# A pause of GpSimd's own between two row gathers and the next two, in the blocks of a graph layer with experts

## The chip, the cores and the metric

One core of one Trainium2 chip runs the whole kernel. The metric is the time of one execution on the device, in microseconds (us). Engines: TensorE (PE, matmuls; PEld its weight loads), VectorE (DVE), ScalarE (ACT), GpSimd (POOL) and SyncE (SP, which here only issues transfers).

## The reference

The inputs are 6250 nodes of 256 features and 200000 edges (source, destination, one of 32 relation types, a weight), sorted by destination. Cut to what matters:

```
xn = layernorm(x)
weight = einsum('rb,bio->rio', w_comp, bases)          # 32 relations from 8 bases
msg = (xn @ weight)[src, rel_type] * edge_weight
gnn = relu(segment_sum(msg, dst))
mix = linear attention over all nodes, layer norm, two dense layers, layer norm, + xn
x = x + gnn + mix
# 8 experts of three dense layers each, weighted by a softmax router, on layernorm(x)
out = x + ffn(layernorm(x))
```

## The kernel before, in words

**Edges as steps.** The sorted edges are cut into chunks of 128, and a chunk that touches several groups of 16 destination nodes is taken once for each. Each such piece is a step. For a step GpSimd gathers the 128 source rows of `xn` (128 x 1 KB) from DRAM into one of the 16 slots of `ring`; TensorE multiplies them with a matrix of 128 x 128 that VectorE has made (`selm`: destination in the group, times relation coefficients), in two halves of two products each; VectorE adds the PSUM result onto a running sum (`acc`, L1306), and SyncE stores every four sums to DRAM (`step_sums`). 16 steps are one iteration (UN = 16); there are 123 iterations, 1968 steps.

**Stages.** 7 iterations run beside the first stage of the mixing (M1_ITS), 8 beside its second stage for the first four tiles; these 15 are FIRST. Then come the blocks: 12 blocks of 9 iterations (BLK), 108 iterations. In a block the steps run between the mixing of the next four tiles of nodes, the product of the aggregated sums with the bases, and (from the second block on) the eight experts on the rows of the block before. Two more blocks without steps end the kernel.

**What sets the order.** Every engine has its own instruction list in an order written out by hand; between the engines there are only counting semaphores. Names that the prediction uses:
- `mm_done` counts multiplied steps and starts at 16, so GpSimd may gather step s + 16 into a slot once step s is multiplied.
- `idx_ready`: VectorE writes the row indices of iteration it + 1 (L1276, `indices`) after the first two accumulations of iteration it. GpSimd waits for it at the start of each iteration.
- `row_in0` to `row_in7`: one for each pair of slots. TensorE waits for a pair before it multiplies its even step (in `step`).
- `wait_apart` (L325) waits for a semaphore, and counts up another, `passed`, behind it.
- `const` on GpSimd is a `Chain`: each of the setup's iotas (L700) waits for the signal of the one before it.
- L1270 is VectorE's product that makes four steps' matrices (`select`); `h_low` (L1005) is the low part of the experts' hidden values. Both read two operands from SBUF.

GpSimd does little else than the gathers: constants at the start, 16 gathers of edge records, and then one loop of 41 turns with three iterations in each, since the index buffer has three parts (SETS = 3).

Of the kernel before, what the change touches and what calls it, by code (L numbers as in the profile page):

```python
# [13 lines left out]
P = 128  # L14
# [28 lines left out]
UN = 16  # L43
# [14 lines left out]
FIRST = M2_AT + 2 * SUP  # L58
ITERS = FIRST + (SUPERS - 1) * BLK
SETS = 3  # L60
# [19 lines left out]
def gps_layer(nc, x, src, dst, etype, eweight, bases, w_comp, Wq, Wk, Wv, Wm, W1, W2, g1, b1, g2, b2,  # L80
              Wr, br, fW1, fb1, fg1, fbe1, fm1, fv1, fW2, fb2, fg2, fbe2, fm2, fv2, Wo, bo, out):
    ctx = ExitStack()
    with ctx:
        sems = {}

        def sem(name):
            if name not in sems:
                sems[name] = ctx.enter_context(nc.semaphore(name))
            return sems[name]
# [3 lines left out]
        def sb(name, shape, dt=F32):  # L93
            place_of[name] = -(-nc.sbuf_base // 32) * 32
            return ctx.enter_context(nc.sbuf_tensor(name, shape, dt))
# [205 lines left out]
        last_i = sb("last_i", [P, 4], I32)  # L301
        zrow = sb("zrow", [P, KH * (P + 1)])
        flag = sb("flag", [1, 1], I32)
        flagf = sb("flagf", [P, 1])


# [18 lines left out]
        def wait_apart(eng, name, value):  # L325


            eng.wait_ge(sem(name), value)
            eng.sem_inc(sem("passed"), 1)
# [22 lines left out]
        def dma_ahead(eng, name, n):  # L352
            eng.dma_start(lead_s[:, 4 * n:4 * n + 4], x[0:1, 0:4]).then_inc(sem(name), DLEAD)
# [339 lines left out]
        @block.gpsimd  # L693
        def _(pool):
            dma_ahead(pool, "s_scat", len(LED_DMA))

            const = Chain(pool, "pool_const")

            def iota(o, pattern, cm=0):
                const(pool.iota(o, pattern, base=0, channel_multiplier=cm, allow_small_or_imprecise_dtypes=True))  # L700

            iota(iota16[:, :], [[1, GN]])
            iota(super_at[:, :], [[SGROUPS, SUPERS]])
            iota(group_no[:, :], [[P, 4]], 1)
            iota(super_no[:, :], [[1, SUPERS]])
            iota(chunk_no[:, :], [[P, CB]], 1)
            iota(slot_no[:, :], [[P, SB]], 1)
            for q in range(4):
                iota(relcol[32 * q:32 * q + 32, :], [[0, 1]], 1)
            pool.wait_ge(sem("dve_const"), 1)  # L710
            const(pool.affine_select(out=ident[:, :], in_=ident[:, :], compare_op=ALU.not_equal, fill=1.0, base=0,
                                     pattern=[[-1, P]], channel_multiplier=1))
            pool.wait_ge(sem("dve_const"), 8)

            const(pool.affine_select(out=rowmask[:, :], in_=rowmask[:, :], compare_op=ALU.is_gt, fill=0.0, base=NODES,
                                     pattern=[[-P, TILES]], channel_multiplier=-1))

            pool.wait_ge(sem("flag_ready"), 1)
            unsorted = pool.value_load(flag[0:1, 0:1], min_val=0, max_val=1)
            with pool.If(unsorted > 0):  # L720
                pool.iota(s_iota, [[1, SORTK]], base=0, channel_multiplier=0,
                          allow_small_or_imprecise_dtypes=True).then_inc(sem("s_const"), 1)
                pool.wait_ge(sem("s_fill"), 3)

                pool.affine_select(out=s_low, in_=s_low, compare_op=ALU.is_gt, fill=0.0, base=0,
                                   pattern=[[1, P]], channel_multiplier=-1).then_inc(sem("s_const"), 1)
                with pool.Fori(0, CHUNKS) as i:
                    wait_apart(pool, "s_recs", i + 1)
                    pool.indirect_dma_start(out=srt, out_offset=bass.IndirectOffsetOnAxis(ap=s_idx, axis=0),
                                            in_=s_rec, in_offset=None).then_inc(sem("s_scat"), 16)  # L730


            pool.wait_ge(sem("rec_ready"), 1)
            with pool.Fori(0, SB // 4) as i:
                for u in range(4):
                    wait_apart(pool, "col_ready", 8 * i + 2 * u + 2)
                    pool.indirect_dma_start(out=irec[:, u, :], out_offset=None, in_=rec,
                                            in_offset=bass.IndirectOffsetOnAxis(ap=colc[:, u:u + 1], axis=0)
                                            ).then_inc(sem(f"irec_in{u}"), 16)
            pool.wait_ge(sem("xn_ready"), 1)  # L740

            def steps(it, u):
                pool.wait_ge(sem("idx_ready"), it + 1)
                for k in range(UN):
                    wait_apart(pool, "mm_done", it * UN + k + 1)
                    pool.indirect_dma_start(out=ring[:, k, :], out_offset=None, in_=xnD,  # L746
                                            in_offset=bass.IndirectOffsetOnAxis(ap=idxc[:, u, k:k + 1], axis=0)
                                            ).then_inc(sem(f"row_in{k // 2}"), 16)

            with pool.Fori(0, ITERS // SETS) as i:  # L750
                for u in range(SETS):
                    steps(SETS * i + u, u)


        @block.scalar
        def _(act):
# [1268 lines left out]
```

## Time and profile before

| | |
|---|---|
| median of 3 runs | 4193.39 us (4190.02 to 4204.43) |
| the profiled execution | 4209.15 us |
| its span, first to last instruction | 4207.4 us |
| TensorE, weight loads busy | 80%, 70% of the span |
| VectorE, ScalarE, GpSimd busy | 54%, 19%, 46% |
| mean granted clock of TensorE | 0.92 of full speed |
| transfers | 864.29 MB, 205 GB/s on the mean |

Busy time is the sum of an engine's instructions, without its register, branch and semaphore instructions and without the issuing of transfers; the gathers, whose descriptors GpSimd itself writes, do count as its busy time. A transfer's own time in flight is not in it. "Idle before" is the time in which an engine did nothing just ahead of an instruction, put to what released it: "issue" where no waiting is seen, "remote" where the releaser is not in the records.

### The profile page before, as it was taken

To read this page: it belongs to the slowest core of one execution; us is meant where nothing else is said; L and a number is where in the kernel's file an instruction comes from. 1 tells how busy PE (TensorE), PEld (TensorE's weight loads), DVE (VectorE), ACT (ScalarE), POOL (GpSimd) and SP (SyncE) were. 2 spreads that over 40 slices of the span, in tenths; PEclk is the share of its full clock that TensorE was granted. 3 is DMA by queue.
4 is the path that set the end of the run, shared out by engine and by line. 5 is a ranking of instruction groups with operands and counts; after the bars stand their busy time and mean duration, and the time that the engine had idled before them with its cause. 6 is when DMAs were issued, how large, how long until landed. Compare 5 with 4: busy or idle time off the path is not lost.

```text
span 4207.4 us, 68614 instructions
## 1 busy us (share of the span) xinstructions
PE 3357.9 (80%) x18778; PEld 2955.5 (70%) x18778; DVE 2255.9 (54%) x6008; ACT 800.3 (19%) x1546; POOL 1949.4 (46%) x2001
## 2 busy tenths in 40 slices
PE   0179976686988889898898888888888888888887
PEld 0157765575877868788787787877877778777675
DVE  5634465555555565555555555555555555555422
ACT  0023420001112121121211212112121221211233
POOL 0132246655555555555555555555454555555100
PEclk9999987887999999999899998998989999899899
DMA  6467776666766667676676766767667676676532
GB/s 195 128 194 237 241 206 189 198 194 207 235 206 219 211 219 239 201 230 208 210 232 208 229 210 209 228 217 226 204 210 231 214 219 216 208 237 207 163 103 80
DMA packets 647245, 864.29 MB, mean 205 GB/s; under 512 B 63829, under 2 KB 524195, under 8 KB 646686
## 3 DMA queue, kind: packets, MB, share of 16 engines
q1 hardware_dynamic: 510962, 549.74, 40.0%
q0 software_dynamic: 95776, 262.27, 21.8%
q10 hardware_dynamic: 40140, 47.81, 3.4%
q8 instruction: 179, 2.93, 0.3%
q14 instruction: 188, 1.54, 0.1%
HBM read 551.97 MB, written 316.84 MB: 206 GB/s over the span
## 4 chain that ended last, share of the span: by engine, by line
PE 53%; issue 11%; DVE 9%; another core or an unknown queue 5%; ACT 3%; DVEq 1%; SPq 0%; DMA 0%; ACTq 0%
PE PS L1674 53%; DVE steps L1306 4%; ACT feed L926 1%; DVE steps L1270 1%; DVE feed L1602 1%; ACT h_high L925 0%; ACT mixbuf L902 0%; DVE h_low L1005 0%; PE PS L1743 0%; ACT mixbuf L896 0%; DVE lst L1415 0%; DVE mixbuf L1437 0%; DVE lnr L1005 0%; DVE mixbuf L1005 0%
## 5 line engine op out<-in xcount | busy, mean ns | idle before, releaser
L746 POOL DMA_INDIRECT steps<-normed_nodes,steps x1968 | 1931.2, 981 | 1781.9 <-PE PS L1674 877.3
L1306 DVE SCALAR_TENSOR_TENSOR steps<-steps,PS 128x256 f32<-128x256 f32 x1968 | 944.7, 480 | 1599.5 <-PE PS L1674 1107.1
L1674 PE MATMUL PS<-steps 128*128 128x128 f32 x7872 | 1267.4, 299 | 316.6 <-issue 133.3
L1674 PEld LDWEIGHTS PS<-steps 128*128 128x128 f32 x7872 | 1169.1, 211 | 422.6 <-issue 257.7
L926 ACT ACTIVATE feed<-PS,bnc 128x512 f32<-128x512 f32 x416 | 319.9, 774 | 825.5 <-PE PS L1674 547.4
L1674 PE MATMUL PS<-bases_s,feed 128*128 128x256 f32 x1664 | 440.7, 408 | 0.0
L1674 PEld LDWEIGHTS PS<-bases_s,feed 128*128 128x128 f32 x1664 | 416.4, 334 | 6.2
L1270 DVE TENSOR_TENSOR steps<-steps 128x512 f32<-128x512 f32 x494 | 337.3, 683 | 0.1
L1674 PE MATMUL PS<-w_one,feed 128*128 128x256 f32 (+1 forms) x1028 | 309.5, 427 | 5.8 <-ACT feed L926 5.8
L925 ACT ACTIVATE h_high<-PS,bnc 128x512 fp32r<-128x512 f32 x208 | 161.6, 777 | 794.5 <-PE PS L1674 724.4
L1674 PE MATMUL PS<-h_high,split_in 128*128 128x512 f32 x832 | 276.0, 458 | 16.8 <-ACT feed L926 16.7
L1674 PE MATMUL PS<-x1t_high,split_in 128*128 128x512 f32 x832 | 261.6, 439 | 2.7 <-DMA w_one<-in_L_ffn_Wo_dram 2.3
L1602 DVE SCALAR_TENSOR_TENSOR feed<-PS,rw,feed 128x256 f32<-128x256 f32 x416 | 181.6, 479 | 111.7 <-PE PS L1674 106.1
L1674 PE MATMUL PS<-w_zero,feed 128*128 128x256 f32 x832 | 226.6, 402 | 6.7 <-ACT feed L926 6.7
L1674 PEld LDWEIGHTS PS<-w_one,feed 128*128 128x128 f32 x1028 | 179.5, 193 | 46.0 <-issue 24.7
L1674 PEld LDWEIGHTS PS<-h_high,split_in 128*128 128x128 f32 x832 | 163.8, 217 | 47.2 <-ACT feed L926 21.3
L1674 PE MATMUL PS<-w_s,mixbuf 128*128 128x256 f32 x416 | 122.7, 446 | 87.5 <-ACT mixbuf L902 50.0
L1674 PEld LDWEIGHTS PS<-wblk,steps 128*128 128x128 f32 x992 | 141.1, 217 | 65.5 <-DVE feed L1524 34.9
L1674 PE MATMUL PS<-wblk,steps 128*128 128x32 f32 x992 | 143.6, 292 | 49.7 <-DVE feed L1524 30.2
L1674 PEld LDWEIGHTS PS<-x1t_high,split_in 128*128 128x128 f32 x832 | 153.2, 202 | 27.0 <-DMA w_one<-in_L_ffn_Wo_dram 2.7
L1674 PEld LDWEIGHTS PS<-w_zero,feed 128*128 128x128 f32 x832 | 154.0, 204 | 25.5 <-ACT feed L926 11.3
L1005 DVE TENSOR_TENSOR h_low<-feed,h_high 128x1024 fp32r<-128x1024 f32 x104 | 127.3, 1224 | 69.1 <-ACT feed L926 63.5
(208 smaller groups left out, 2881.3 us busy)
## 6 DMA issues: line engine op xcount, KB each, us to landing
step_sums<-steps SPq DMA_DIRECT2D x492, 512.0 KB
split_in<-expert_split SPq DMA_DIRECT2D x104, 1024.0 KB
feed<-step_sums SPq DMA_DIRECT2D x416, 128.0 KB
steps<-step_types SPq DMA_DIRECT2D x125, 256.0 KB
steps<-normed_nodes,steps POOLq DMA_INDIRECT x1968
mixbuf<-mix_hidden SPq DMA_DIRECT2D x53, 256.0 KB
w_zero<-in_L_ffn_Wo_dram SPq DMA_DIRECT2D x52, 256.0 KB
w_one<-in_L_ffn_Wo_dram SPq DMA_DIRECT2D x52, 256.0 KB
```

Of the source, the lines that this page charges most:

```text
L746: pool.indirect_dma_start(out=ring[:, k, :], out_offset=None, in_=xnD, in_offset=bass.IndirectOffsetOnAxis(ap=idxc[:, u, k:k + 1], axis=0) ...
L925: act.activation(h1_high[:, k, :], bank(b0 + k), ACT.Relu, bias=bias, scale=scale)
L926: act.activation(o[:, k, :], bank(b0 + k), ACT.Relu, bias=bias, scale=scale).then_inc(sem(f"f_h{s}"), 1)
L1005: return dve.tensor_tensor(o, a, b, op)
L1270: dve.tensor_tensor(selm[:, q % 2, :, :, :], hot[:, s, :].unsqueeze(3).to_broadcast([P, BATCH, GN, BASES]), coef[:, s, :].unsqueeze(2).to_ ...
L1306: dve.scalar_tensor_tensor(acc[:, k % ACCR, :], acc[:, (k - 1) % ACCR, :], keepc[:, k:k + 1], PS[:, slot(k):slot(k) + C], ALU.mult, ALU.ad ...
L1602: dve.scalar_tensor_tensor(oacc[:, j, :], o_part(j), rw[:, EXPERTS * j + e:EXPERTS * j + e + 1], oacc[:, j, :], ALU.mult, ALU.add).then_in ...
L1674: return pe.matmul(o, a, b, start=start, stop=stop)
```

## The change

A buffer `hold` of 128 x 8 words is added in SBUF. In `steps`, when `turn` is given, GpSimd does two things ahead of each even gather, behind the wait for `mm_done`: it clears `hold` with a memset that counts up the semaphore `held`, and waits until `held` has reached this memset's own number. Nothing reads `hold`. The one loop over all iterations becomes two: the first over FIRST = 15 iterations without `turn`, the second over the other 108 with it.

```diff
+        hold = sb("hold", [P, 8])
...
-            def steps(it, u):
+            def steps(it, u, turn=None):
                 pool.wait_ge(sem("idx_ready"), it + 1)
                 for k in range(UN):
                     wait_apart(pool, "mm_done", it * UN + k + 1)
+                    if turn is not None and k % 2 == 0:
+                        pool.memset(hold[:, :], 0.0).then_inc(sem("held"), 1)
+                        wait_apart(pool, "held", turn * (UN // 2) + k // 2 + 1)
                     pool.indirect_dma_start(out=ring[:, k, :], out_offset=None, in_=xnD,
                                             in_offset=bass.IndirectOffsetOnAxis(ap=idxc[:, u, k:k + 1], axis=0)
                                             ).then_inc(sem(f"row_in{k // 2}"), 16)
 
-            with pool.Fori(0, ITERS // SETS) as i:
+            with pool.Fori(0, FIRST // SETS) as i:
                 for u in range(SETS):
                     steps(SETS * i + u, u)
-
+            with pool.Fori(0, (ITERS - FIRST) // SETS) as i:
+                for u in range(SETS):
+                    steps(SETS * i + FIRST + u, u, SETS * i + u)
```

## Rows read from the trace of the kernel before

**Rows 1.** The page: GpSimd's busy time, and the shares of the chain by engine.
```profile
PE 3357.9 (80%) x18778; PEld 2955.5 (70%) x18778; DVE 2255.9 (54%) x6008; ACT 800.3 (19%) x1546; POOL 1949.4 (46%) x2001
...
PE 53%; issue 11%; DVE 9%; another core or an unknown queue 5%; ACT 3%; DVEq 1%; SPq 0%; DMA 0%; ACTq 0%
```

**Rows 2.** By line, L746: durations (ns), its idle time by releaser, who waited for it.
```profile
L746 POOL DMA_INDIRECT steps<-normed_nodes,steps x1968: 940/946/1991, 226.8 to 3924.3; - x197
...
  PE PS L1674: 877.3, 521
  issue: 440.5, 1298
  DVE steps L1276: 371.6, 96
...
  PEld PS L1674: 7.1, 1
  PE PS L1674: 6.9, 1
```

**Rows 3.** By line, L1306: durations (ns), first and last start (us).
```profile
L1306 DVE SCALAR_TENSOR_TENSOR steps<-steps,PS x1968: 461/481/483, 245.2 to 3952.8; 128x256 f32<-128x256 f32 x197
```

**Rows 4.** Windows by block, L746: stretch, its length, busy time (count), clock, DMA share, GB/s.
```profile
800.00:1036.00 236.00, 138.48 (x146) 0.80 0.66 203
1036.00:1302.00 266.00, 143.13 (x146) 0.92 0.69 216
...
sum 3151.00, POOL 1685.78; mean POOL 140.48
```

**Rows 5.** Timeline, all engines, 2041 to 2053 us: start, length, instructions [idle before, releaser].
```profile
2042.12 0.17 DVE L1276 CAST steps<-steps 128x16 int32 x1
...
2043.18 0.94 POOL L746 DMA_INDIRECT steps<-normed_nodes,steps  x1 [3.98 <-DVE steps L1276]
...
2044.43 0.94 POOL L746 DMA_INDIRECT steps<-normed_nodes,steps  x1 [0.30 <-issue]
...
2051.72 0.69 DVE L1270 TENSOR_TENSOR steps<-steps 128x512 f32<-128x512 f32 x1
...
2052.05 1.18 POOL L746 DMA_INDIRECT steps<-normed_nodes,steps  x1 [0.30 <-issue]
```

**Rows 6.** Timeline of GpSimd, the first 30 us.
```profile
0.30 0.10 POOL L2015 MEMSET const-float32-0.0<- 128x1 f32 x1 [0.30 <-issue]
...
1.36 0.70 POOL L353 DMA_DIRECT2D lead_s<-in_x_dram  x1 [0.85 <-POOLq L2015]
2.16 0.18 POOL L700 IOTA iota<- 128x16 f32 x1
2.41 0.16 POOL L700 IOTA super_at<- 128x13 f32 x1
...
4.35 0.29 POOL L711 TENSOR_SCALAR_AFFINE_SELECT ident<-ident 128x128 f32<-128x128 f32 x1 [0.16 <-DVE headmask L1045]
```

**Rows 7.** Transfers by line: count, size, median us from issue to landing.
```profile
mixbuf<-in_x_dram SPq DMA_DIRECT2D x8, 768.0 KB, 6.1
```

**Rows 8.** Groups of VectorE, 800 to 3951 us: busy us, mean ns, idle before.
```profile
L1270 DVE TENSOR_TENSOR steps<-steps 128x512 f32<-128x512 f32 x432 | 294.9, 683 | 0.1
...
L1005 DVE TENSOR_TENSOR h_low<-feed,h_high 128x1024 fp32r<-128x1024 f32 x88 | 107.7, 1224 | 5.6
```

**Rows 9.** Waits: who waited for whom, us in total, times, longest us.
```profile
DVE steps L1306 <- remote: 326.2, 82, 17.7
...
ACT feed L926 <- remote: 160.2, 18, 13.6
...
PE PS L1743 <- DMA feed<-in_x_dram: 4.3, 1, 4.3
...
PE PS L1674 <- DMA w_one<-in_L_ffn_Wo_dram: 2.3, 1, 2.3
```

## The prediction

> **What bounds the kernel now.** I read the chain of work that ended last first, because it says which engine's delay would count. TensorE carries 53% of it, issue time 11%, VectorE 9%, and GpSimd is not in it [rows 1]. GpSimd is busy for 46% of the span, nearly all of it with the gathers of line 746. So the change touches an engine off the path, and the question is how much it can be slowed before it comes onto it.
>
> The view by line for 746 gives both sides [rows 2]. Before the 1968 gathers GpSimd sat idle for 877.3 us waiting for TensorE to free a ring slot, for 371.6 us waiting for VectorE's next list of indices, and 440.5 us in short issue gaps. The other way round almost nobody waits for a gather: one weight load and one matmul, 7.1 and 6.9 us, in the whole run. Inside the first block the same view lists no waiter at all. The ring explains it: gather s+16 is issued as soon as step s is multiplied, so each gather has the time of nearly 16 steps to land. The last gather starts at 3924.3 us [rows 2] and the last accumulation, which uses it, at 3952.8 us [rows 3]: 28.5 us later.
>
> How fast the ring turns is read from the windows by block [rows 4]. Windows cut at the block borders hold 145 gathers or so; the twelve blocks take 3151 us for 1728 steps, so a pair of steps (one handshake in the new code) takes 3151/864 = 3.65 us. The first block, which has no experts, is the quickest: 236 us, 236/72 = 3.28 us a pair. These two are the rates GpSimd has to keep.
>
> **What the change adds.** Nothing is removed and no transfer is added or moved past another on a queue. In 108 iterations with 8 pairs each, 864 memsets are added, and 864 waits for the memset's own signal. The waits for `mm_done` and `idx_ready` stay. The one loop of 41 turns becomes two, of 5 and 36, with the same three iterations in each turn: one more loop start, counted as nothing. Behind the waiting memset only the next gather of the same engine is queued; behind that, TensorE, by `row_in`, 16 steps later.
>
> The price of one handshake, when GpSimd has slots in hand and does not wait for TensorE anyway. Before, gathers run back to back: 0.95 us of gather and 0.30 us to the next one [rows 5], so a pair takes 2.50 us; 1298 of the 1968 follow within such an issue gap [rows 2]. As a gather behind another starts after 0.30 us and one that waited for a signal only after 0.89 us (below), I take it that part of a gather's start is done ahead while the one before runs; the new wait stops that. The new sequence for a pair is
> - gather, gap, gather: 0.95 + 0.30 + 0.95 = 2.20 us;
> - the gap before the memset. After the one other DMA that GpSimd issues, which ends at 1.36 + 0.70 = 2.06 us, the next operation starts at 2.16 us [rows 6]: 0.10 us;
> - the memset of 128x8 words. None of this shape is in the trace; those of 128x1 take 0.10 us [rows 6]. 0.10 us;
> - from the memset's end to the next gather's start. The nearest row is a gather that waited for a signal on an empty queue: the index cast ends at 2042.12 + 0.17 = 2042.29 us and the gather starts at 2043.18 us [rows 5]: 0.89 us. (The chain of iotas, each waiting for the signal of the one before, shows 2.16 + 0.18 = 2.34 to 2.41 us, 0.07 us [rows 6]; so the signal itself is cheap and the 0.89 us is mainly the gather's own start.)
>
> Together 3.29 us. The mean gather is 981 ns against a median of 946 [rows 2], which adds 0.07 us a pair: 3.36 us, 0.79 us more than before on the same footing, 864 x 0.79 = 683 us of GpSimd's time in all. Of this nothing lies on the path as long as 3.36 stays under 3.65: GpSimd then uses 92% of its time in the blocks. In the first block it does fall behind, by (3.36 - 3.28) x 72 = 6 us, against the 28.5 us lead, of which the landing takes some. The landing of a gather is in no view; the nearest, a load of 768 KB, takes 6.1 us from issue [rows 7], so about 22 us may be lost before TensorE waits. In the later blocks GpSimd wins back 0.29 us a pair. So I cost the handshakes at nothing; the cover is the ring, and were it gone they would cost up to 683 us.
>
> Bounds of one handshake. Below, nothing or less: if the wait overlapped the gather's start completely, a pair stays at 2.50 us and the time does not move. Above: a gap of 0.30 instead of 0.10 us, and a memset held off by a whole VectorE operation, 0.68 us for L1270, the commonest with two SBUF operands [rows 8]: 3.36 + 0.20 + 0.68 = 4.24 us. I take 3.36, since each of its terms has its own row, and the memsets, iotas and the select of [rows 6] all take 0.10 to 0.29 us.
>
> Gathers are in fact stretched when VectorE is at such an operation: the one at 2052.05 us takes 1.18 us, and an L1270 of 0.69 us began at 2051.72 [rows 5]. The Trainium skill ("GPSIMD Engine Reference", Specifications) says that GpSimd shares its SBUF interfaces with VectorE and contends with instructions that have two SBUF inputs. By that rule, and the trace agrees with it as far as that pair of rows goes, a memset can be held for the rest of the operation; if it met each one in full the upper bound would be the sum. VectorE's big ones in the blocks, L1270 with 294.9 us and h_low with 107.7 us [rows 8], take 403/3151 = 13% of the time, so a memset that comes at any moment meets one in 13% of cases and waits about half of it: 0.05 us on the mean.
>
> The other direction, memsets holding VectorE: 864 x 0.10 = 86 us of memset, 13% of it beside such an operation, 11 us, and VectorE is 9% of the chain: 1 us.
>
> **Sum.** Blocks +0 to +1 us. The profiled execution took 4209.15 us (span 4207.4 us and 1.8 us around it), so it would become 4210; it lies 15.8 us above the median of 4193.39 us of the timed runs, to which the forecast is made: 4194 us.
>
> **The rivals.**
> (a) GpSimd becomes the bound: slower. This decides from 3.65 us a pair. The handshake would need a gap of 0.30 (+0.20) and a memset with its write and signal as long as the select's 0.29 (+0.19) [rows 6]: 3.75 us, 864 x 3.75 = 3240 us for the blocks against 3151, +89 us, less the 22 us of lead: +67, 4260 us. For it: the forecast sits at 92% of the limit, and a wait after descriptor work by this engine is nowhere in the trace. Against it: the small operations of [rows 6]. At the upper bound, 4.24 us, it would be 3663 - 3151 - 22 = +490 us, 4683 us; that needs every memset to meet a full VectorE operation, against 13% of the time.
> (b) Spaced gathers help the other transfers: faster. A burst brings 128 KB per 1.25 us, 105 GB/s; afterwards 128 KB per 1.68 us, 78 GB/s. An unknown releaser holds VectorE's L1306 for 326.2 us and ScalarE's L926 for 160.2 us [rows 9], and has 5% of the chain [rows 1], 210 us. If these were transfers and a tenth were saved: -21 us, 4172 us. Against it: L1306 waits for TensorE most of the time, and TensorE's waits put down to a named DMA are 2.3 and 4.3 us [rows 9]; the unknown releaser is more likely a matmul that is missing from the records.
> (c) The handshake does not do what it says: the wait is over before the sequencer reaches it, a pair stays near 2.50 us. Then the time is 4193 us too, and only the profile could tell it from the forecast.
>
> **How the numbers follow.** Forecast 0.66, (a) 0.21 (its upper bound 0.03 of that), (b) 0.10, (c) 0.03. About 0.3%, 12.6 us, is what a measurement can tell from no change here; the runs before spread from 4190.02 to 4204.43. The forecast and (c) are within 0.3%, but for 0.02 that I give to noise on the faster side. Faster 0.12, same 0.67, slower 0.21. The range: 4178 us takes half of (b), and 4240 us takes in the mild part of (a), in which the pair is near 3.7 us; left out are the heavy part of (a), about 0.12, and half of (b), 0.05. The likeliest case alone is 4186 to 4206 us.
>
> **What would show each step.** A MEMSET group of 864 on GpSimd with a mean near 100 ns; if the mean is above 300, the price is wrong. The gather behind a memset begins about 0.9 us after it, and the pair in a burst takes 3.3 to 3.4 us. Idle time charged to TensorE before line 746 shrinks, and a new idle time charged to the memset, near 864 x 0.89 = 770 us, appears. The waiters of line 746 stay at a few us and the chain has no GpSimd. The forecast is wrong if TensorE waits for gathers, if GpSimd enters the chain, or if the windows of the blocks, the first above all, grow by more than 12 us in sum.

## The result, and the profile after

The changed kernel takes 3945.28 us (median of 4, 3931.65 to 3952.15) against 4198.91 us before (median of 4, 4190.02 to 4210.12) on the same chip: a ratio of 0.939, 95% interval 0.936 to 0.943. No change was forecast, with 4178 to 4240 us as the range: wrong by 249 us. The gain is not there on every chip: on two others, where the kernel before takes 3741 to 3745 us, the same change makes it slower, 1.037.

The page of the changed kernel, lines that answer to [rows 1]:

```profile
PE 3248.9 (82%) x18778; PEld 2880.1 (73%) x18778; DVE 2252.9 (57%) x6008; ACT 800.9 (20%) x1546; POOL 2088.2 (53%) x2865
...
PE 47%; issue 14%; DVE 7%; DMA 5%; ACT 3%; POOL 3%; DVEq 1%; SPq 0%; POOLq 0%; ACTq 0%
```

GpSimd, absent from the chain before, now has 3% of it, and transfers 5%. Its timeline shows the new pair:

```profile
2000.19 0.12 POOL L749 MEMSET hold<- 128x8 f32 x1
2001.12 0.95 POOL L751 DMA_INDIRECT steps<-normed_nodes,steps  x1 [0.81 <-POOL hold L749]
2002.38 0.95 POOL L751 DMA_INDIRECT steps<-normed_nodes,steps  x1 [0.30 <-issue]
2003.32 0.13 POOL L749 MEMSET hold<- 128x8 f32 x1
2004.26 0.95 POOL L751 DMA_INDIRECT steps<-normed_nodes,steps  x1 [0.81 <-issue]
```

From 2001.12 to 2004.26 us is 3.14 us a pair. And the view by line (L751 is the old L746) shows what GpSimd waited for and, in the last two lines, who now waited for gathers; [rows 2] had 6.9 and 7.1 us there, once each:

```profile
  PE PS L1681: 516.7, 499
  issue: 475.3, 1126
  POOL hold L749: 261.3, 323
  DVE steps L1283: 69.0, 10
...
  PE PS L1681: 86.7, 45
  PEld PS L1681: 32.6, 12
```

Windows at the block borders (stretch, length, GpSimd's busy time, clock, DMA share, GB/s), against 3151 us in [rows 4]; the first window is the first block:

```profile
787.50:1019.50 232.00, 141.61 (x144) 0.82 0.67 208
...
sum 2912.50, POOL 1725.71; mean POOL 575.24
```

The blocks are 238.5 us shorter, the stretch ahead of them 12.5 us (800.00 to 787.50 us) and the end 6 us: 257 us of span (4207.4 to 3950.4 us). The gain is in the blocks, and TensorE gets it although it now waits for gathers. The same windows over all engines, before and after:

```profile
800.00:3951.00 3151.00, 2673.42 (x14976) 2396.18 (x14977) 1786.64 (x4680) 570.20 (x982) 1685.78 (x1715) 0.92 0.69 216
...
787.50:3700.00 2912.50, 2574.00 (x14983) 2327.92 (x14982) 1783.97 (x4680) 570.60 (x982) 1830.88 (x2582) 0.94 0.74 234
```

The first busy time is TensorE's. Of the 238.5 us, 139 us are idle time of TensorE that went away (478 to 339 us); the other 99 us are the same products done in less busy time, at a mean granted clock of 0.94 instead of 0.92. What went away is in [rows 9]: VectorE's L1306 waited 326.2 us for an unknown releaser there. The same line of the changed kernel:

```profile
DVE steps L1313 <- remote: 92.7, 15, 17.8
```

**Where the time had been: TensorE's signals came late.** The timeline of the kernel before, all engines, 2017 to 2023 us:

```profile
2017.12 0.95 POOL L746 DMA_INDIRECT steps<-normed_nodes,steps  x1 [0.30 <-issue]
...
2017.83 1.05 PE L1674 MATMUL PS<-steps 128*128 128x128 f32 x8
...
2018.37 0.94 POOL L746 DMA_INDIRECT steps<-normed_nodes,steps  x1 [0.30 <-issue]
...
2019.62 0.95 POOL L746 DMA_INDIRECT steps<-normed_nodes,steps  x1 [0.31 <-issue]
...
2022.17 1.00 DVE L1306 SCALAR_TENSOR_TENSOR steps<-steps,PS 128x256 f32<-128x256 f32 x2 [4.38 <-PE PS L1674]
2022.18 0.37 ACT L935 COPY feed<-PS 128x256 f32<-128x256 f32 x1 [5.97 <-remote]
2022.79 0.94 POOL L746 DMA_INDIRECT steps<-normed_nodes,steps  x1 [2.23 <-PE PS L1674]
```

The eight products of two steps end at 2018.88 us. VectorE, which needs only these, starts at 2022.17, 3.29 us later, ScalarE starts with it, and GpSimd's gather, which also waits for TensorE, 0.62 us later. The records of semaphore updates in the same trace, which the views don't print, say the same: four increments of `mm_done`, due at 2018.44, 2018.89, 2020.42 and 2021.73 us, are recorded at 2021.995, 2022.054, 2022.215 and 2022.333 us. GpSimd's last gather before that ends at 2020.57 us, so these signals did not come at the moment it stopped, but 1.4 to 1.8 us later.

I counted this for whole traces. "Late" is a recorded increment of a semaphore that only TensorE increments, over 100 ns behind the last matmul that could have made it; an episode is a group of late ones less than 0.7 us apart. In the blocks of the kernel before there are 978 late ones of TensorE in 477 episodes (from the matmul's end to the record, a late one comes 1.1 us late in the median and 9.8 us at most), and none of VectorE or ScalarE. In the changed kernel there are 223 in 191. Not all updates are recorded (2508 and 2037 of some 2958 of TensorE's, and 2972 and 2965 of VectorE's 4679), so the counts are lower bounds.

A second measure needs no record of a signal: how long VectorE stood idle in the blocks ahead of a pair's first sum although its own last work and the pair's last product had both ended (idle times under 0.35 us left out). That is 432 us before, at 211 of 864 pairs, and 64 us at 50 pairs after. So late signals cost VectorE time, and the change took most of that away.

### The profile page after: what moved, and what is told of

Same layout as the page of the kernel before. It is cut to its first block, busy times and chain, and to the rows that moved or that the text cites. A ratio compares the mean times of both kernels' runs of the same rounds, so it can differ in the third digit from the quotient of the medians.

```text
span 3950.4 us, 71207 instructions
## 1 busy us (share of the span) xinstructions
PE 3248.9 (82%) x18778; PEld 2880.1 (73%) x18778; DVE 2252.9 (57%) x6008; ACT 800.9 (20%) x1546; POOL 2088.2 (53%) x2865
## 4 chain that ended last, share of the span: by engine, by line
PE 47%; issue 14%; DVE 7%; DMA 5%; ACT 3%; POOL 3%; DVEq 1%; SPq 0%; POOLq 0%; ACTq 0%
PE PS L1681 46%; DMA steps<-normed_nodes,steps 5%; DVE steps L1313 3%; POOL steps L751 2%; ACT feed L933 2%; DVE steps L1277 1%; ACT h_high L932 1%; DVE h_low L1012 1%; DVE feed L1609 0%; ACT mixbuf L909 0%; PE PS L1750 0%; ACT mixbuf L903 0%; DVE steps L1258 0%; SPq L542 0%; DVE lst L1422 0%
## 5 line engine op out<-in xcount | busy, mean ns | idle before, releaser
L751 POOL DMA_INDIRECT steps<-normed_nodes,steps x1968 | 1964.2, 998 | 1338.8 <-PE PS L1681 516.7
L1681 PE MATMUL PS<-steps 128*128 128x128 f32 x7872 | 1228.2, 293 | 273.5 <-DMA steps<-normed_nodes,steps 85.2
L1681 PEld LDWEIGHTS PS<-steps 128*128 128x128 f32 x7872 | 1134.6, 205 | 369.7 <-issue 245.1
L1277 DVE TENSOR_TENSOR steps<-steps 128x512 f32<-128x512 f32 x494 | 337.8, 684 | 0.1
L1681 PE MATMUL PS<-x1t_high,split_in 128*128 128x512 f32 x832 | 252.6, 426 | 2.4 <-DMA w_one<-in_L_ffn_Wo_dram 2.4
L1681 PE MATMUL PS<-w_zero,feed 128*128 128x256 f32 x832 | 217.8, 390 | 6.7 <-ACT feed L933 6.7
L1681 PEld LDWEIGHTS PS<-w_one,feed 128*128 128x128 f32 x1028 | 178.5, 192 | 45.1 <-issue 24.3
L1681 PE MATMUL PS<-wblk,steps 128*128 128x32 f32 x992 | 134.6, 282 | 44.7 <-DVE feed L1531 39.5
L1012 DVE TENSOR_TENSOR h_low<-feed,h_high 128x1024 fp32r<-128x1024 f32 x104 | 127.3, 1224 | 69.3 <-ACT feed L933 63.7
L1681 PEld LDWEIGHTS PS<-feed,w_one 128*128 128x128 f32 x1176 | 142.9, 192 | 23.7 <-issue 23.7
```

The source lines that it names most:

```text
L1012: return dve.tensor_tensor(o, a, b, op)
L1277: dve.tensor_tensor(selm[:, q % 2, :, :, :], hot[:, s, :].unsqueeze(3).to_broadcast([P, BATCH, GN, BASES]), coef[:, s, :].unsqueeze(2).to_ ...
L1681: return pe.matmul(o, a, b, start=start, stop=stop)
```

## The experiments

The chips differ, so each ratio is to the kernel before on the same chip. A is the chip of the measurement above, B that of e and f, C of g, D of h, E of i. The time of the kernel before is in brackets. "Idle" is the second measure above, in us. The changed kernel itself was not run on B; f4 is the nearest to it there.

```
kernel                 chip         ratio (95%)            late, episodes   idle   what is done
before                 A (4199)     1                      978, 477         432
changed                A            0.939 (0.936-0.943)    223, 191         64     8 stops an iteration
e1 wait four back      B (4274)     1.001 (0.999-1.004)    976, 458         510    no stop
e2 every fourth        B            0.983 (0.979-0.986)    1058, 565        496    4 stops an iteration
e3 long, one back      B            0.986 (0.982-0.990)    994, 496         445    0.33 us filler, no stop
e4 indices early       B            0.965 (0.962-0.969)    1053, 500        370    no memset at all
f1 filled pause        B (4267)     0.983 (0.979-0.986)    1064, 750        457    gap 0.75 us, filled, no stop
f2 long stop, fourth   B            0.964 (0.961-0.967)    857, 430         274    4 long stops
f3 every gather        B            1.033 (1.029-1.036)    2, 2             3      16 stops
f4 everywhere          B            0.928 (0.924-0.932)    377, 307         98     8 stops, all iterations
g0 changed again       C (3745)     1.037 (1.034-1.039)    0                6
g1 everywhere, early   C            1.038 (1.036-1.041)    0                12
g2 six stops           C            1.029 (1.027-1.031)    0                5
g3 no gathers          C            0.991 (0.988-0.994)    0                11
h0 before again        D (3741)     1.000 (0.998-1.002)    0                2
h1 no gathers again    D            0.990 (0.987-0.993)    0                11
h2 changed             D            1.037 (1.032-1.042)    0                6
h3 filled pause        D            1.017 (1.014-1.020)    0                9
i0 before              E (4285)     one run, 4260 us       1016, 489        473
i1 no gathers          E            0.878 (0.871-0.884)    0                11
```

My theory after the result: on this chip an unbroken run of gathers holds TensorE's signals up, and the stop lets them through. The rival: a lower rate of gathers, or the memsets themselves, help.

**e1, the stop taken away.**

```diff
-                        pool.memset(hold[:, :], 0.0).then_inc(sem("held"), 1)
+                        pool.memset(hold[:, k // 2:k // 2 + 1], 0.0).then_inc(sem("held"), 1)
                         wait_apart(pool, "held", turn * (UN // 2) + k // 2 + 1)
...
+            pool.sem_inc(sem("held"), 4)
```

> The same number of memsets and waits as the changed kernel (864 each), but each wait asks for the memset four pairs earlier, so it is always over already; the memset is of one word, in eight places in turn. Theory (the changed kernel is faster because the wait stops GpSimd between two gathers and the next two, and in that pause the signals of the other engines, held up by an unbroken run of gathers, get through): the run of gathers is broken only by the memset's 0.12 us, so most of the gain is lost: 4120 to 4200 us against 4199 before and 3945 changed. Rival 1 (the memsets themselves, or the two loops, bring the gain): 3945 us. Rival 2 (gathers that come more slowly help in proportion to their spacing): a pair takes about 2.7 us against 2.5 before and 3.13 changed, a third of the gain, 4115 us.

Measured 1.001: as many memsets and waits, and nothing gained. The rival that the memsets or the two loops bring the gain is out. Spacing is not tested by this run: its memset fits into the 0.30 us between two gathers, and a back-to-back pair stays at 2.50 us instead of the 2.7 expected.

**e2, half as many stops** (`k % 4 == 0`).

> The memset and the wait for it only ahead of every fourth gather: runs of at most four gathers, 432 pauses. Theory: in the trace of before, signals are late more often the longer the run of gathers has lasted (prompt for 0.63, 0.59, 0.30, 0.19 of TensorE's increments at places 1 to 4 of a run, 0.05 from place 6), so runs of four give part of the gain, but GpSimd needs 5.6 us per four steps instead of 6.3 and is no longer the bound (27.0 us per iteration now, 25.1 needed): 3960 to 4080 us. Rival (what helps is only a lower rate of gathers): half of the gain, 4070 us. If being bound by GpSimd costs more than the signals give, it is faster than the changed kernel: 3900 us.

Measured 0.983, less gain than either side expected.

**e3, filler of 0.33 us instead of a stop.** The wait stands ahead of a memset of 258 words and asks for that of the pair before.

```diff
-                        pool.memset(hold[:, :], 0.0).then_inc(sem("held"), 1)
                         wait_apart(pool, "held", turn * (UN // 2) + k // 2 + 1)
+                        pool.memset(zrow[:, :], 0.0).then_inc(sem("held"), 1)
...
+            pool.sem_inc(sem("held"), 1)
```

> Ahead of each even gather a memset of 258 words (about 0.3 to 0.4 us), with a wait for the memset of the pair before, so that GpSimd need not come to a stop: the pause between gathers is filled with other work of GpSimd and its front end may run ahead. Theory in its first form (writing descriptors without a break holds the signals up, any break helps): a gap of 0.4 to 0.5 us instead of 0.30, between half and all of the gain, 3950 to 4080 us. Theory in its second form (GpSimd has to come to a stop, with nothing queued): near before, 4150 to 4200 us.

Measured 0.986 with 994 late: nearer to the second form, GpSimd has to come to a stop. The gap between a pair and the next was 0.49 us, only a little longer, so f1 was to repeat it at the changed kernel's length.

**e4, indices two iterations ahead.**

```diff
-                    indices(it + 1, u + 1)
+                    indices(it + 2, u + 2)
```

> The kernel before with one edit: VectorE writes the row indices two iterations ahead instead of one, no memset and no wait. GpSimd then loses its 371.6 us of waiting for indices (96 times), after which it had a backlog to work off in one run. Theory: fewer and shorter runs of gathers, since they follow TensorE's steps more evenly, so signals are less late: 4050 to 4180 us. Rival (the index wait does not make the runs; late signals do, and they feed on themselves): 4190 to 4200 us, no change.

Measured 0.965, inside the theory's range, but with 1053 late increments: it doesn't make signals prompt. They cost less: VectorE's idle time behind them is 370 us, against 445 to 510 us in e1, e2 and e3 on the same chip. Why is not shown.

**f1, a filled pause.**

```diff
+                        wait_apart(pool, "held", turn * (2 * UN) + 4 * (k // 2) + 4)
+                        pool.memset(zrow[:, :], 0.0).then_inc(sem("held"), 1)
+                        pool.memset(kvmask[:, :], 0.0).then_inc(sem("held"), 1)
+                        pool.memset(rowmask[:, :], 0.0).then_inc(sem("held"), 1)
                         pool.memset(hold[:, :], 0.0).then_inc(sem("held"), 1)
-                        wait_apart(pool, "held", turn * (UN // 2) + k // 2 + 1)
...
+            pool.sem_inc(sem("held"), 4)
```

> Ahead of each even gather four memsets of finished buffers (258, 128, 49 and 8 words, about 0.33 + 0.22 + 0.15 + 0.12 us), with a wait for those of the pair before: a pause between pairs of about 1.0 to 1.1 us, as long as the changed kernel's (1.06 us from a gather's end to the next one's start), but filled, and GpSimd's front end does not come to a stop. Theory P (what TensorE's signals need is about 1 us without descriptors being written, whatever fills it): late increments of TensorE in the blocks fall from some 980 to about 220, as in the changed kernel, and the time to 0.93 to 0.95 of before. Theory Q (GpSimd has to come to a stop, with no gather queued behind): 0.98 to 1.00 of before, with about 1000 late increments.

Its timeline of GpSimd:

```profile
2011.73 0.94 POOL L754 DMA_INDIRECT steps<-normed_nodes,steps  x1 [0.30 <-issue]
2012.66 0.34 POOL L750 MEMSET zrow<- 128x258 f32 x1
2012.92 0.23 POOL L751 MEMSET kvmask<- 128x128 f32 x1
2013.06 0.17 POOL L752 MEMSET rowmask<- 128x49 f32 x1
2013.13 0.13 POOL L753 MEMSET hold<- 128x8 f32 x1
2013.42 0.95 POOL L754 DMA_INDIRECT steps<-normed_nodes,steps  x1 [0.16 <-issue]
2014.68 0.95 POOL L754 DMA_INDIRECT steps<-normed_nodes,steps  x1 [0.30 <-issue]
```

From a gather's end at 2012.67 to the next start at 2013.42 are 0.75 us, which is also the median of all blocks; expected were 1.0 to 1.1, and the changed kernel has 0.93 us (2003.33 to 2004.26). A pair takes 2.95 us (2011.73 to 2014.68) instead of 3.14. So the run misses its aim by 0.18 us: gap and rate are not the same as the changed kernel's. The ratio is 0.983 with 1064 late, as theory Q says. Between e3's filled gap of 0.49 us and this one of 0.75 us neither the late ones nor the time moved (994 and 1064, 0.986 and 0.983), so the gap doesn't act in proportion. Most likely the stop does it; that the last 0.18 us of gap do it is not ruled out by any run.

**f2, f3, f4: long stops ahead of every fourth gather, stops ahead of each gather, stops in all iterations.**

> Ahead of every fourth gather three memsets of 258 words, each waited for: a pause of about 2.1 us after four gathers, so GpSimd's rate is that of the changed kernel (6.7 us for four gathers against 6.3) but the runs are four long. If the lower rate is what helps (GpSimd becomes the bound and TensorE waits for rows, evenly): 0.94 to 0.96 of before. If short runs are what helps: 0.97 to 1.00, with 700 or more late increments.

> The memset and its wait ahead of every gather: no runs at all, GpSimd needs 0.95 + 1.06 = 2.01 us a step, 32.2 us an iteration. TensorE's late increments fall to under 100, but GpSimd bounds the blocks: 108 x 32.2 = 3478 us against 3151, 1.07 of before. If late signals cost nothing, the same time; the run separates the price of the bound from that of the signals by the count of late increments and by the waits for rows.

> The changed kernel with the memset and wait in all 123 iterations, one loop. The first 15 iterations take 54 us (seven) and 25 us (eight) each; runs of 5 and more occur there too, with TensorE's increments prompt in under a fifth of cases at such places. Theory: 5 to 25 us less than the changed kernel, 0.934 to 0.940 of before. If the first stage is bound by ScalarE and VectorE, no change: 0.939.

f2, 0.964 with 857 late, lies between its two answers and tells them apart badly. f3 is the clearest in signals: with no gather ever behind another, 2 late increments are left of about 1000, and TensorE pays in waits for rows instead:

```profile
L751 POOL DMA_INDIRECT steps<-normed_nodes,steps x1968: 943/954/1977, 226.8 to 4153.3; - x197
...
  PE PS L1681: 429.8, 205
```

GpSimd becomes the bound, at 1.95 us a step (3366 us of blocks for 1728 steps) instead of the 2.01 expected, and the kernel is 1.033 and not 1.07 of before. f4 measured 0.928, better than the 0.934 expected at best; but that is a ratio on chip B against 0.939 on chip A, and in time it is 3954 us against 3945, so it isn't shown to be faster than the changed kernel. What f4 shows is the comparison with f1 on one chip: stops and a gap of 0.93 us give 0.928 with 377 late, a filled gap of 0.75 us 0.983 with 1064.

**g, another chip, another sign.**

> The changed kernel, unedited, beside the others on one chip: 0.93 to 0.94 of before. The chips differ: before took 4199 us with the first measurement and 4267 to 4274 us with the experiments.

> Memset and wait in all 123 iterations, and the row indices written two iterations ahead. The early indices alone gave 0.965, the stops alone 0.928. If they act on the same thing (fewer gathers queued behind one another): 0.925 to 0.930, nothing added. If GpSimd, which is the bound in the stretches where TensorE waits for rows (113.5 us), catches up sooner: 0.90 to 0.92.

> In all iterations six stops of 16 gathers instead of eight (ahead of gathers 0, 3, 6, 8, 11, 14): runs of three and two. GpSimd needs 20 + 6 x 0.63 = 23.8 us an iteration instead of 25.0. Theory (late signals come from gathers queued behind one another, and runs of four had 857 to 1058 late increments, runs of two 223 to 377): 500 to 800 late ones and 0.94 to 0.96. If being bound by GpSimd is what is left: 0.915 to 0.925.

> The kernel before without the gathers of the blocks: GpSimd still waits for each slot, TensorE doesn't wait for rows and multiplies what the ring held before, so the sums of the blocks are left out of the computation. All else stays, the stores of 2 MB an iteration too. Theory: TensorE's late increments fall to 0 to 20 and the time to 0.87 to 0.91 of before, which is all that late signals and the gathers' transfers can cost. Rival (late signals are an effect of TensorE's own stalls on VectorE, not of GpSimd): several hundred late increments stay and the time is 0.97 to 1.00.

g0, g1 and g2 missed their expectations. g3 has the theory's count of late ones (0) and the rival's time, so it fits neither. On chip C the kernel before takes 3745 us, no trace has a late increment, and every kernel with stops is slower; fewer stops (g2) cost less. Without the gathers there is 1% to win, not 10%.

**h, the same on chip D, with a trace of the kernel before.**

> The kernel before, unedited, for its trace on this run's chip. So far: chips on which it takes 4190 to 4297 us, with TensorE's increments late 978 times in the blocks of the one trace, and one chip on which it takes 3745 us and three traces of other kernels show none late. If the chip decides: where it takes about 3745 us, 0 late increments in spite of runs of five gathers and more; where it takes 4200 or more, some 900 to 1100.

> Without the gathers of the blocks, as g3_no_gathers (the sums of the blocks are left out of the computation). On a chip like the one of g3: 0.99 of before, none late. On a chip where before takes 4200 us or more: if the gathers make the signals late, 0 to 20 late and about 3700 us, 0.87 to 0.89 of before; if such a chip is slow for another reason, late increments stay and the ratio is above 0.95.

> The changed kernel on the same chip: 1.03 to 1.04 of before where that takes about 3745 us; 0.92 to 0.94 where it takes 4200 us or more.

> The filled pause again: the changed kernel's rate of gathers without a stop, 0.98 where before took 4267 us. On a chip without late signals both pay only for the lower rate: 1.03 to 1.04, the same as the changed kernel. If the changed kernel's loss on such a chip is the stop itself and not the rate, the filled pause costs less: 1.00 to 1.02.

h0 had 0 late increments. Here is the place of the timeline shown above (same block, same steps) in the kernel before on chip D:

```profile
1812.03 1.21 POOL L746 DMA_INDIRECT steps<-normed_nodes,steps  x1 [0.30 <-issue]
...
1812.94 1.05 PE L1674 MATMUL PS<-steps 128*128 128x128 f32 x8
1813.54 0.95 POOL L746 DMA_INDIRECT steps<-normed_nodes,steps  x1 [0.30 <-issue]
...
1814.12 1.00 DVE L1306 SCALAR_TENSOR_TENSOR steps<-steps,PS 128x256 f32<-128x256 f32 x2 [1.70 <-PE PS L1674]
...
1814.79 0.95 POOL L746 DMA_INDIRECT steps<-normed_nodes,steps  x1 [0.30 <-issue]
```

The products end at 1813.99 and VectorE starts at 1814.12 us, 0.13 us later instead of 3.29, with the gathers running behind one another just the same (up to 91 in one unbroken run in this trace, 13 on chip A). Its windows from the first block's start to the last one's end:

```profile
sum 2734.10, POOL 1706.24; mean POOL 853.12
```

That is 2734/864 = 3.16 us a pair, against 3.65 in [rows 4], and close to the 3.14 us that GpSimd needs for a pair with a stop. In h2, the changed kernel on this chip, TensorE waits for rows and the blocks take longer:

```profile
  PE PS L1681: 110.6, 71
  PEld PS L1681: 32.7, 21
...
sum 2876.50, POOL 1716.23; mean POOL 1716.23
```

The filled pause (h3) costs 1.7% here, the changed kernel 3.7%; their pairs take 2.95 and 3.13 us, so the difference can be the rate alone.

**i, the gathers taken away on a chip of the slow kind.**

> The kernel before, unedited, for its trace on this run's chip: about 3745 us and no late increments of TensorE, or 4190 us and more with about 1000 late ones; if the two always go together, the late increments are what sets the two kinds of chip apart.

> Without the gathers of the blocks (their sums are left out of the computation), in the hope of a chip on which before takes 4190 us or more. There: if gathers make the signals late, 0 to 20 late and about 3700 us, 0.87 to 0.89 of before; if such a chip is slow without them too, above 0.95. On a chip of the other kind 0.99, as twice before.

Chip E is of that kind: 4260 us with 1016 late increments. Without the gathers of the blocks there are none, as expected if the gathers make them, and the time is 3756.85 us, 0.878, within 51 us of the same kernel on chips C and D (3709.38 and 3706.78 us). In the blocks nothing is left of the difference between the chips, 2712 us on E and 2717 us on D. The 45 us that remain lie ahead of the blocks (797 us against 752), where this kernel still gathers, and there the trace of E has 77 late increments and that of D 5. So the gathers make the late signals, on some chips, and the late signals come with nearly all of the difference between the kinds: 4285 - 3757 = 528 us here, 3745 - 3709 = 36 us on C. The stores of 2 MB an iteration were still there, but the gathers' own transfers went with them; what GpSimd's writing of descriptors does and what the transfers do is not separated by this run, nor by another. Slower transfers are not what sets the chips apart: the packets of GpSimd's queue take 21.8% of 4207.4 us on A and 24.3% of 3733.3 us on D, 917 and 907 us.

## Why the prediction was wrong, point by point

- **The price of the handshake: right.** 3.14 us a pair against 3.29 from the rows (3.36 with stretching). Gap before the memset about 0 instead of 0.10, memset 0.12 to 0.13 instead of 0.10, from its end to the gather 0.81 instead of 0.89 us. The memsets added 107 us of busy time, not 86. The idle time charged to the memset is 261.3 us and not 770: 323 waits of 0.81 us, since only part of the memset's signals are recorded; the rest stands under "issue".
- **VectorE holding the memset: small**, as taken, but not for the reason given. Median 120, longest 398 ns. The 73 memsets that lay wholly inside one of VectorE's two-operand products (L1277, the old L1270) and the 40 inside an `h_low` (L1012) took 130 ns at most; the 16 that took over 200 ns each lay beside L1253 or L1558, which the prediction did not have. The bound of 0.68 us more for each was far off.
- **"Almost nobody waits for a gather", hence the cover of the ring, hence handshakes costed at nothing: the step that failed.** It was true of the data and taken as true of the engine. That nothing waits for gathers by semaphore doesn't mean that they delay nobody: they delayed TensorE's signals to VectorE, ScalarE and GpSimd, 978 late ones in the blocks, and VectorE stood idle for 432 us behind products that had ended. With the handshake that is 64 us, and the blocks are 238.5 us shorter; the sum had no term for it.
- **The rate of 3.65 us a pair as the one GpSimd has to keep: wrong for the same reason.** It was TensorE's rate with late signals. Where they come in time, on chip D, the blocks run at 3.16 us (h0), and GpSimd at 3.14 us without stretching becomes a bound: the changed kernel runs at 2912.5/864 = 3.37 us, with 86.7 us of TensorE's waits for gathers.
- **"The unknown releaser is more likely a matmul that is missing from the records"** was in rival (b), and half right: the releaser was TensorE, with an update that came late. I read the row as a gap of the profile, not of the signal. The sign stood in the trace: an L1306 that waits 4.38 us "for PE" although its matmuls ended 3.3 us before its start.
- **Rival (b), spaced gathers help the transfers: right side, another mechanism.** The packets of GpSimd's queue took 21.8% of 4207.4 us before and 23.0% of 3950.4 us after, 917 and 909 us, so the transfers hardly got quicker. In f1 the gathers are spaced too, if by 0.18 us less, and only 1.7% is gained.
- **Rival (a), GpSimd becomes the bound, slower: it happened on chips C and D**, at +3.7%, not because the handshake cost more than 3.65 us but because the ring there turned faster than I could see from one chip.
- Not settled: what in GpSimd's queue holds TensorE's signals, whether it is the stop or the gap's last 0.18 us that lets them through, and why only on some chips. The count of late signals doesn't order the kernels on chip B: e4 (0.965) and f2 (0.964) have about as many as before. VectorE's idle time behind them does, but for f3, which GpSimd bounds: 510 us (e1, 1.001), 496 (e2, 0.983), 457 (f1, 0.983), 445 (e3, 0.986), 370 (e4, 0.965), 274 (f2, 0.964) and 98 (f4, 0.928), with e2, e3 and f1 within each other's noise. That the gain of the changed kernel is all from prompt signals rests on e1, i1, these idle times and the counts together, not on one run.

## What to carry to other kernels

When an engine waits for another, compare its start with the end of the very instruction that it waits for; a wait far longer than that is a late signal, and the engine that is "off the path" may cause it. An engine that nobody waits for can still set the pace, so a slack computed from the current rate isn't slack once something else is relieved. Measure a gain that has no mechanism in the profile on a second chip before keeping it: here 6% faster and 4% slower are the same edit.

## What the runs showed of the hardware

The five chips fall into two kinds for this kernel: 4190 to 4297 us (A, B, E) and 3731 to 3751 us (C, D). On A, B and E, while GpSimd gathered with indices, TensorE's semaphore increments came late, up to 9.8 us in the kernel before, in groups; those of VectorE and ScalarE did not (0 of some 3000 and 600 recorded). A wait for GpSimd's own signal with a gap of 0.93 us ahead of every pair helped, a gap of 0.75 us filled with memsets did not. On these chips 15 to 31% of TensorE's updates in the blocks are missing from the records of the kernels with gathers, and 24 to 48% of VectorE's; on C and D under 2% of either. Without the gathers of the blocks (i1) none of TensorE's is missing on E either, so the loss of records comes with the gathers, too.
